# A cross-attention and expert layer on one core: the first six periods laid out anew, the router as one operand

## The chip, the core and the metric

One NeuronCore of a Trainium2 chip runs the whole program. The metric is the device time of the program in microseconds, the median over its runs; the kernel before takes 211.32 us (three runs: 210.55 to 213.79).

## What is computed

Eight sequences (batches) of 256 tokens, width 128, all in float32:

```python
scores = jnp.einsum('bhqd,bhkd->bhqk', q, k) / jnp.sqrt(jnp.float32(dh))   # 8 heads of 16
attn = jax.nn.softmax(scores, axis=1)                                     # over the heads
ctx = jnp.einsum('bhqk,bhkd->bhqd', attn, v)
...
logits = jnp.einsum('btd,de->bte', x, Wr) + br                            # 8 experts
topv, topi = jax.lax.top_k(logits, K)                                     # K = 2
gates = jax.nn.softmax(jnp.where(sel_mask, logits, neg_inf), axis=-1)
h = jax.nn.relu(jnp.einsum('btd,edh->bteh', x, W1) + b1)                  # hidden 256
out = jnp.einsum('bte,bteh,ehd->btd', gates, h, W2) + jnp.einsum('bte,ed->btd', gates, b2)
...
x = x + xattn(layernorm(x), context, context)
x = x + ffn(layernorm(x))
```

The softmax runs over the eight heads, not over the keys, so each pair of query and key has its own maximum and sum over 8 values. Every token goes through all eight experts; the gates of six are zero.

## The kernel before

Each batch's 256 tokens are two tiles of 128. Its attention is four units u = 0 to 3 (key tile by query tile). A unit is a chain over the engines: **scores** (TensorE, 1,024 columns into one of two PSUM pairs of banks), **head_max** (VectorE, maximum over the heads), **subtract_max** (TensorE adds minus the maximum to all heads in PSUM), **exponentiate** (ScalarE), **head_sum** (GpSimd, three additions; for the four units of batch 0 TensorE with eight identity matmuls, line 351), **invert_sum** (ScalarE, exp(-ln)), **normalize** (VectorE). After four units come **attend_values** (32 small matmuls), take_heads (ScalarE), **project_out**, then add_residual and ln2 (VectorE), ln2_end (GpSimd), make_x1n (ScalarE), **transpose_x1n** (TensorE), take_x1T_hi (ScalarE) and x1T_low (VectorE). With these come **route** (TensorE), take_logits, choose_experts, make_gates, transpose_gates (VectorE, gap_power on ScalarE), and eight times **expert_up** (six matmuls, line 403), relu (ScalarE), **expert_down** (eight, line 416), add_expert (VectorE), with gated_b2 and add_b2 once.

Scores, router and first expert layer use float32r, TensorE's reduced form, on a high and a low part (hi, lo) of one or both operands; three products stand for one float32 product. For the scores the parts of K and Q are spilled to DRAM and loaded again as stacks in which the parts of two heads lie under each other (k_stack, q_stack); batch 0 goes another way, with k_first and q_wide straight from PSUM (first_scores). SyncE's queue issues the spills, the loads of the stacks, w1, w2, most of the context and the stores of the output, strictly in the order written; each spill waits for both parts, each load for its spill. ScalarE's queue issues the attention's weights, the rest of x, two contexts and the small weights at the start.

The order of the work is written out by hand for each engine. Every engine runs its list strictly in order and waits on semaphores. The function beginning() of each engine holds the first six periods (0 to 5) as one list; from period 6 on period(i) (lines 418 onwards for TensorE) repeats a fixed pattern with the attention of batch i - 2, the end of that of i - 3, the experts 0 to 5 of batch i - 4 and 6 and 7 of batch i - 5. PERIODS is 13, and the last ones run out. The experts of batch 0 and of batch 1 up to 5 up, 4 down, and the attention up to unit 3 of batch 3 stand in beginning().

Other places that the change touches: keep_warm(n) (line 263) issues n dummy matmuls of 128 columns (each shows as two instructions on line 265) into the score bank of odd units. There are 12 of them ahead of beginning() and 5, 1 and 2 in its first lines. route (line 291) has three matmuls per token tile, each with the 128 tokens as weights and 8 columns of the router's weights (wr_hi or wr_lo) moving. ln1 (VectorE, line 833) makes mean and variance of a run of tiles, ln1_rstd_of and ln1_rest (GpSimd) the rest. GpSimd clears q_stack[1], v_pad and later q_stack[0] with memsets (lines 1223, 1224, 1187).

## Time and profile before

| | |
|---|---|
| median of three runs | 211.32 us (210.55 to 213.79) |
| profiled execution | 210.83 us, its span 209.0 us |
| TensorE matmul busy | 199.0 us, 95% of the span |
| TensorE weight load busy | 176.3 us, 84% |
| VectorE busy | 166.0 us, 79% |
| ScalarE busy | 132.3 us, 63% |
| GpSimd busy | 110.0 us, 53% |
| TensorE in the chain that ended last | 91% |

The span runs from the first to the last instruction of the program on the core. The chain that ended last is followed back from the last instruction, at each step to what released it. Ends of matmuls are modelled, since they are pipelined: a matmul group's distance from start to start is what it costs the ones behind it.

### The profile page before, as it was taken

How to read it: one execution, taken by the hardware profiler on the slowest of the kernel's cores; microseconds unless marked ns; L12 is line 12 of the kernel's file. 1: busy time of each engine (PE TensorE's matmuls, PEld its weight loads, DVE VectorE, ACT ScalarE, POOL GpSimd, SP SyncE). 2: the span in 40 equal slices, each digit the busy share in tenths (PEclk: the TensorE clock that was granted, in tenths of full speed). 3: DMA queues.
4: the chain of work that ended last, by engine and by line, in shares of the span. 5: the costliest groups of instructions: out<-in, count | busy, mean ns of one | idle time of the engine just before them, and what ended most of it. 6: DMA issues, size and time to landing. Idle time of an engine off the chain costs nothing.

```text
span 209.0 us, 4976 instructions
## 1 busy us (share of the span) xinstructions
PE 199.0 (95%) x1752; PEld 176.3 (84%) x1752; DVE 166.0 (79%) x445; ACT 132.3 (63%) x316; POOL 110.0 (53%) x132
## 2 busy tenths in 40 slices
PE   6999888698999999999999999999999999999994
PEld 6846775686899889997999799988998999789993
DVE  5398779889789999988888988798989978365542
ACT  2236847796578858687668767575767685345541
POOL 8603657869795475439661966285738672010000
PEclk9999999999999999999999999999999999999999
DMA  6549695725434233424241306050000000000000
GB/s 195 137 137 291 178 266 161 206 86 159 109 102 100 78 100 105 102 75 104 98 106 53 124 14 183 13 175 4 0 3 25 0 2 28 0 3 2 28 0 25
DMA packets 20248, 18.70 MB, mean 89 GB/s; under 512 B 1760, under 2 KB 18688, under 8 KB 20224
## 3 DMA queue, kind: packets, MB, share of 16 engines
q1 hardware_dynamic: 17472, 16.91, 28.2%
q10 hardware_dynamic: 2752, 1.48, 2.7%
q8 instruction: 14, 0.23, 0.4%
q14 instruction: 10, 0.08, 0.1%
HBM read 11.83 MB, written 6.55 MB: 88 GB/s over the span
## 4 chain that ended last, share of the span: by engine, by line
PE 91%; DVE 3%; ACT 2%; issue 1%; POOL 1%; DVEq 0%; POOLq 0%; ACTq 0%
PE y_ps L416 28%; PE h_ps L403 21%; PE score_ps L343 7%; PE misc_ps L362 6%; PE score_ps L331 6%; PE h_ps L351 4%; PE score_ps L265 3%; PE misc_ps L300 2%; PE misc_ps L383 2%; PE score_ps L320 2%; PE score_ps L403 2%; PE misc_ps L371 1%; PE misc_ps L270 1%; PE misc_ps L309 1%; PE misc_ps L289 1%
## 5 line engine op out<-in xcount | busy, mean ns | idle before, releaser
L670 ACT ACTIVATE hT<-h_ps,b_sb 128x256 f32<-128x256 f32 x118 | 49.4, 470 | 34.5 <-PE h_ps L403 33.4
L416 PE MATMUL y_ps<-w_sb,hT 128*128 128x128 f32 x512 | 68.4, 276 | 0.0
L416 PEld LDWEIGHTS y_ps<-w_sb,hT 128*128 128x128 f32 x512 | 63.3, 191 | 3.4 <-issue 2.0
L1152 POOL TENSOR_TENSOR half_sum<-e_sb 128x512 f32<-128x512 f32 x28 | 36.9, 1320 | 34.0 <-ACT e_sb L642 33.6
L911 DVE TENSOR_TENSOR attn<-e_sb,e_rcp 128x1024 f32<-128x1024 f32 x32 | 42.8, 1341 | 3.5 <-ACT e_rcp L653 3.3
L903 DVE TENSOR_REDUCE shift_m<-score_ps 128x128 fp32r<-128x1024 f32 x32 | 38.7, 1213 | 2.4 <-PE score_ps L331 1.2
L403 PE MATMUL h_ps<-x1T_hi,w_lo 128*128 128x256 f32 x118 | 37.7, 320 | 1.3 <-ACT hT L670 0.6
L642 ACT ACTIVATE e_sb<-score_ps 128x1024 f32<-128x1024 f32 x32 | 32.8, 1024 | 5.4 <-PE score_ps L343 5.2
L974 DVE SCALAR_TENSOR_TENSOR acc<-y_ps,gates,acc 128x128 f32<-128x128 f32 x96 | 29.0, 343 | 8.3 <-PE y_ps L416 6.9
L403 PE MATMUL h_ps<-x1T_lo,w_hi 128*128 128x256 f32 x118 | 33.1, 280 | 0.0
L403 PE MATMUL h_ps<-x1T_hi,w_hi 128*128 128x256 f32 x118 | 33.0, 279 | 0.0
L1154 POOL TENSOR_TENSOR quarter_sum<-half_sum 128x256 f32<-128x256 f32 x28 | 27.5, 982 | 2.2
L403 PEld LDWEIGHTS h_ps<-x1T_hi,w_lo 128*128 128x128 f32 x118 | 22.3, 189 | 4.3 <-issue 2.0
L403 PEld LDWEIGHTS h_ps<-x1T_lo,w_hi 128*128 128x128 f32 x118 | 22.4, 190 | 0.3
L403 PEld LDWEIGHTS h_ps<-x1T_hi,w_hi 128*128 128x128 f32 x118 | 22.3, 189 | 0.0
L343 PE MATMUL score_ps<-shift_m,neg_ident 128*128 128x512 f32 x64 | 21.5, 417 | 0.0
L331 PE MATMUL score_ps<-q_stack,k_stack 128*128 128x256 f32 x112 | 19.6, 299 | 1.1 <-issue 1.1
L1157 POOL TENSOR_TENSOR e_sum<-quarter_sum 128x128 f32<-128x128 f32 x28 | 16.6, 592 | 2.2
L1163 POOL TENSOR_TENSOR ln_rstd<-ln_var,neg_half 128x2 f32<-128x2 f32 x8 | 5.7, 708 | 21.2 <-DVE ln_var L870 21.2
L331 PEld LDWEIGHTS score_ps<-q_stack,k_stack 128*128 128x128 f32 x112 | 15.1, 190 | 1.5 <-issue 1.5
L362 PE MATMUL misc_ps<-attn,v_pad 128*32 128x256 f32 x256 | 15.5, 382 | 0.6 <-issue 0.6
L362 PEld LDWEIGHTS misc_ps<-attn,v_pad 128*32 128x32 f32 x256 | 7.7, 109 | 5.9 <-issue 1.0
(113 smaller groups left out, 286.8 us busy)
## 6 DMA issues: line engine op xcount, KB each, us to landing
k_scratch<-k_parts SPq DMA_DIRECT2D x14, 256.0 KB, 2.6
k_stack<-k_scratch SPq DMA_DIRECT2D x14, 256.0 KB, 4.0
q_stack<-q_scratch SPq DMA_DIRECT2D x28, 128.0 KB, 2.7
q_scratch<-q_parts SPq DMA_DIRECT2D x7, 256.0 KB, 2.5
w_sb<-in_w SPq DMA_DIRECT2D x1, 1024.0 KB, 6.5
out_y<-y_out SPq DMA_DIRECT2D x8, 128.0 KB, 1.9
x_all<-in_x ACTq DMA_DIRECT2D x1, 768.0 KB, 6.0
ctxT<-in_ctx_t SPq DMA_DIRECT2D x1, 640.0 KB, 5.5
```

The lines of the kernel that those rows point to most:

```text
L331: mm = nc.tensor.matmul(score_ps[:, u % 2, 2 * j * P:(2 * j + 2) * P], k_stack[:, b % 2, j, kt * P:(kt + 1) * P], q_stack[:, b % 2, j, :, ...
L343: mm = nc.tensor.matmul(score_ps[:, u % 2, half * BANK:(half + 1) * BANK], neg_ident[:], m4, start=False, stop=True, skip_group_check=True)
L362: mm = nc.tensor.matmul(misc_ps[32 * g:32 * g + 32, 0:S], v_pad[:, b % 4, kt, h, :], attn[:, b % 2, kt, h, :], start=(odd == 0 and kt == 0 ...
L403: mm = nc.tensor.matmul(hidden(j)[:, c * S:(c + 1) * S], w[:, e, c * P:(c + 1) * P], xt[:, b % 2, :], start=(k == 0), stop=(k == 2))
L416: mm = nc.tensor.matmul(y_ps[:, j % 2, t * D:(t + 1) * D], hT[:, j % 2, c, t * P:(t + 1) * P], w2_sb[:, e * HC + c, :], start=(c == 0), st ...
L642: nc.scalar.activation(e_sb[:, u, :], score_ps[:, u % 2, :], ACT.Exp, scale=SCALE).then_inc(exp_made, 1)
L670: op = nc.scalar.activation(hT[:, j % 2, c, :], hidden(j)[:, c * S:(c + 1) * S], ACT.Relu, bias=b1_sb[:, e * HC + c:e * HC + c + 1])
L903: nc.vector.tensor_reduce(shift_m[:, u % 2, :], score_ps[:, u % 2, :].rearrange("p (h q) -> p q h", h=H), AX.X, ALU.max).then_inc(max_made, 1)
L911: nc.vector.tensor_tensor(attn[:, b % 2, kt, :, qt * P:(qt + 1) * P], e_sb[:, u, :].rearrange("p (h q) -> p h q", h=H), e_rcp[:, u, :].uns ...
L974: op = nc.vector.scalar_tensor_tensor(out=dst, in0=y_ps[:, j % 2, t * D:(t + 1) * D], scalar=gates[:, b % 2, t, e:e + 1], in1=src[:, t, :] ...
L1152: nc.gpsimd.tensor_tensor(half_sum[:], e[:, 0:HQ // 2], e[:, HQ // 2:HQ], ALU.add).then_inc(sum_step, 1)
L1154: nc.gpsimd.tensor_tensor(quarter_sum[:], half_sum[:, 0:HQ // 4], half_sum[:, HQ // 4:HQ // 2], ALU.add).then_inc(sum_step, 1)
```

## The change

Router: wr_hi and wr_lo lie side by side in one tile wr_pair. For each token tile one matmul multiplies x1T_hi by both (16 columns), a second adds x1T_lo times the high part to the first 8. take_logits adds the two halves and the bias in two operations with a semaphore between (logits_step) where it had one. This holds for all batches.

SyncE's queue: w1 goes out ahead of every spill, behind two waits for inputs of ScalarE's queue; then both spills (K, Q) of a batch go ahead of both stack loads, for batches 1 and 2, and the rest of the context goes out between batch 1's loads and batch 2's spills.

beginning() is written anew on all four engines. On TensorE the dummies take their PSUM place and a wait as arguments, and stand in ten places behind the first twelve (27 dummies; before in three, 8). Batch 1's units stand wholly ahead of attend_values(0), and three units of batch 2 stand at least in part ahead of expert_up(0, 0). ln1 works on one batch at a time. GpSimd's memset of q_stack[1] moves behind the first ln1_rest. The shapes of k_first and q_wide get a dimension of 1, the counts of the waits stay the same in effect, and period(i) keeps its order.

```diff
 # route
-                    for k, (xt, w) in enumerate(((x1T_hi, wr_lo), (x1T_lo, wr_hi), (x1T_hi, wr_hi))):
-                        mm = nc.tensor.matmul(misc_ps[:, S + t * E:S + (t + 1) * E], xt[:, b % 2, tok], w[:],
-                                              start=(k == 0), stop=(k == 2), skip_group_check=True)
+                    nc.tensor.matmul(misc_ps[:, at:at + 2 * E], x1T_hi[:, b % 2, tok], wr_pair[:].rearrange("p k e -> p (k e)"),
+                                     start=True, stop=False, skip_group_check=True)
+                    mm = nc.tensor.matmul(misc_ps[:, at:at + E], x1T_lo[:, b % 2, tok], wr_pair[:, 0, :],
+                                          start=False, stop=True, skip_group_check=True)
 # take_logits
-                nc.vector.tensor_tensor(logits[:], misc_ps[:, S:S + TT * E].rearrange("p (t e) -> p t e", e=E),
-                                        br_sb[:].unsqueeze(1).to_broadcast([P, TT, E]), ALU.add).then_inc(logits_made, 1)
+                nc.vector.tensor_tensor(logits_part[:], parts[:, :, 1, :], br_sb[:].unsqueeze(1).to_broadcast([P, TT, E]),
+                                        ALU.add).then_inc(logits_step, 1)
+                dve.wait_ge(logits_step, b + 1)
+                nc.vector.tensor_tensor(logits[:], parts[:, :, 0, :], logits_part[:], ALU.add).then_inc(logits_made, 1)
 # SyncE
+            sp.wait_ge(x1_in, 16)
+            sp.wait_ge(ctx_in[1], 16)
+            sp.dma_start(w1_sb[:], w1.rearrange("e d h -> d e h")).then_inc(w1_in, 16)
             spill_k(1)
-            sp.dma_start(w1_sb[:], w1.rearrange("e d h -> d e h")).then_inc(w1_in, 16)
+            spill_q(1)
             load_k_stack(1)
-            spill_q(1)
             load_q_stack(1)
+            sp.dma_start(ctxT[:, 3:B, :], ...)
             spill_k(2)
-            sp.dma_start(ctxT[:, 3:B, :], ...)
+            spill_q(2)
             load_k_stack(2)
-            spill_q(2)
             load_q_stack(2)
```

TensorE's list, up to the first experts, as it stands after the change (kw is keep_warm):

```
project_k(0) project_v(0) kw(2) transpose_xn(0) kw(2) project_q(0) project_k(1) first_scores(0,0) project_k(2)
transpose_xn(1) first_scores(0,1) subtract_max(0,0) project_q(1) kw(3) first_scores(0,2) subtract_max(0,1)
head_sum(0,0) subtract_max(0,2) first_scores(0,3) head_sum(0,1) transpose_xn(2) subtract_max(0,3) project_v(1)
head_sum(0,2) scores(1,0) project_q(2) head_sum(0,3) project_v(2) subtract_max(1,0) scores(1,1) kw(2)
scores(1,2) kw(2) subtract_max(1,1) kw(2) subtract_max(1,2) scores(1,3) attend_values(0) scores(2,0)
subtract_max(1,3) project_out(0) kw(3) scores(2,1) subtract_max(2,0) project_k(3) kw(5) transpose_xn(3) kw(4)
transpose_x1n(0) scores(2,2) subtract_max(2,1) route(0) expert_up(0,0) project_q(3) scores(2,3)
subtract_max(2,2) expert_up(0,1) expert_down(0,0) attend_values(1) expert_down(0,1) project_out(1)
expert_up(0,2) project_k(4) kw(2) expert_up(0,3) expert_down(0,2) subtract_max(2,3) expert_up(0,4)
transpose_x1n(1) expert_down(0,3) scores(3,0) route(1) expert_up(0,5) project_v(3) ...
```

The same of VectorE (new), ScalarE (new) and GpSimd (new):

```
VectorE: ln1(1) spread_q(0,0) ln1_end(1) spread_q(0,1) head_max(0,0) k_lo(1) ln1(2) head_max(0,1) q_lo(1)
split_wr head_max(0,2) ln1(3) k_lo(2) ln1(4) head_max(0,3) normalize(0,0) normalize(0,1) head_max(1,0) q_lo(2)
normalize(0,2) normalize(0,3) head_max(1,1) head_max(1,2) ln1(5) head_max(1,3) normalize(1,0) head_max(2,0)
add_residual(0) ln2(0) head_max(2,1) k_lo(3) ln1(6) normalize(1,1) x1T_low(0) head_max(2,2) take_logits(0)
normalize(1,2) normalize(1,3) q_lo(3) choose_experts(0) make_gates(0) transpose_gates(0) add_expert(0,0)
add_residual(1) ln2(1) head_max(2,3) ... head_max(3,1) make_gates(1) transpose_gates(1) normalize(2,2)
add_expert(0,6) k_lo(5) normalize(2,3) add_expert(0,7) ...
ScalarE: take_xnT(0) take_v(0) take_k_first(0) take_k_hi(1) take_xnT(1) exponentiate(0,0) take_q_hi(1)
make_xn(2) take_k_hi(2) exponentiate(0,1) ... exponentiate(1,0) exponentiate(1,1) take_v(2) exponentiate(1,2)
invert_sum(1,0) split_w1(3) take_heads(0) exponentiate(1,3) invert_sum(1,1) take_k_hi(3) exponentiate(2,0)
make_x1n(0) invert_sum(1,2) take_xnT(3) take_x1T_hi(0) exponentiate(2,1) invert_sum(1,3) relu(0,0) ...
GpSimd: memset v_pad, iota, ln1_rstd_of(0), memset q_stack[0], ln1_rstd_of(1), ln1_rest(2), memset q_stack[1],
ln1_rest(3), ln1_rest(4), split_w1(0..2), head_sum(1,0) head_sum(1,1) head_sum(1,2) ln2_end(0) head_sum(1,3) ...
```

## Rows read from the trace of the kernel before

**Rows 1.** The page's strips of 40 slices: TensorE busy tenths, and its granted clock
```profile
PE   6999888698999999999999999999999999999994
...
PEclk9999999999999999999999999999999999999999
```

**Rows 2.** Busy time by stretch: stretch, its length, then each engine's busy us
```profile
9.38:39.06 29.68, 25.40 (x174) 18.09 (x175) 24.42 (x58) 17.37 (x40) 15.05 (x20) 1.00 0.73 202
39.06:81.44 42.38, 41.72 (x376) 36.99 (x377) 38.21 (x92) 31.05 (x76) 30.23 (x37) 1.00 0.39 114
81.44:209.00 127.56, 124.45 (x1160) 113.96 (x1158) 98.99 (x283) 81.42 (x198) 57.69 (x63) 1.00 0.17 48
```

**Rows 3.** TensorE's waits, 7 to 83 us: who waited for whom, total, times, longest
```profile
PE misc_ps L283 <- ACT x1n L596: 1.4, 1, 1.4
PE score_ps L331 <- issue: 1.1, 1, 1.1
```

**Rows 4.** Timeline of TensorE, a steady router: start, us, line, operation
```profile
86.03 0.25 PE L300 MATMUL misc_ps<-wr_lo,x1T_hi 128*128 128x8 f32 x1
...
86.70 0.37 PE L403 MATMUL h_ps<-x1T_hi,w_lo 128*128 128x256 f32 x1
```

**Rows 5.** VectorE's line 918, take_logits: ns min/median/max
```profile
L918 DVE TENSOR_TENSOR logits<-misc_ps,br_sb x8: 161/176/177, 41.7 to 191.3; 128x16 f32<-128x16 f32 x8
```

**Rows 6.** The page's groups: busy us and mean ns, idle before
```profile
L911 DVE TENSOR_TENSOR attn<-e_sb,e_rcp 128x1024 f32<-128x1024 f32 x32 | 42.8, 1341 | 3.5 <-ACT e_rcp L653 3.3
L903 DVE TENSOR_REDUCE shift_m<-score_ps 128x128 fp32r<-128x1024 f32 x32 | 38.7, 1213 | 2.4 <-PE score_ps L331 1.2
...
L642 ACT ACTIVATE e_sb<-score_ps 128x1024 f32<-128x1024 f32 x32 | 32.8, 1024 | 5.4 <-PE score_ps L343 5.2
```

**Rows 7.** Timeline of TensorE, the beginning
```profile
7.32 1.28 PE L265 MATMUL score_ps<-ident 128*128 128x128 f32 x10
...
23.37 1.95 PE L351 MATMUL h_ps<-e_sb,ident 128*128 128x128 f32 x16
26.41 0.71 PE L331 MATMUL score_ps<-q_stack,k_stack 128*128 128x256 f32 x4 [1.09 <-issue]
...
30.92 1.93 PE L362 MATMUL misc_ps<-attn,v_pad 128*32 128x256 f32 x32 [0.62 <-issue]
...
39.06 0.38 PE L403 MATMUL h_ps<-x1T_hi,w_lo 128*128 128x256 f32 x1 [0.47 <-DVE x1T_lo L875]
...
81.44 0.38 PE L276 MATMUL misc_ps<-ident,xn 128*128 128x128 f32 x2
```

**Rows 8.** Timeline of GpSimd
```profile
3.40 1.88 POOL L1224 MEMSET v_pad<- 128x2048 f32 x1
```

**Rows 9.** Timeline of VectorE, the beginning
```profile
4.98 0.31 DVE L843 TENSOR_SCALAR ln_var<-ln_mv 128x2 f32<-128x2 f32 x1
...
11.21 0.42 DVE L875 TENSOR_TENSOR k_parts<-h_ps,k_parts 128x256 fp32r<-128x256 f32 x1
...
71.22 1.25 DVE L943 TENSOR_SCALAR gap_exp<-gap_exp 128x2 f32<-128x2 f32 x1
```

**Rows 10.** Timeline of SyncE's queue: DMA issues
```profile
13.04 0.62 SPq L244 DMA_DIRECT2D w_sb<-in_w  x1
...
16.85 0.43 SPq L201 DMA_DIRECT2D q_scratch<-q_parts  x1
22.11 1.76 SPq L223 DMA_DIRECT2D q_stack<-q_scratch  x4
```

**Rows 11.** The page's DMA issues: KB each, us to landing
```profile
q_scratch<-q_parts SPq DMA_DIRECT2D x7, 256.0 KB, 2.5
```

**Rows 12.** TensorE in the chain that ended last: start, us, line, instructions
```profile
84.68 0.70 PE h_ps L403 x6
85.38 0.89 PE y_ps L416 x8
...
95.22 1.86 PE misc_ps L362 x32
```

More of the change, by code:

```diff
@@ L262, in _, with keep_warm @@
         def _(pe):
-            def keep_warm(n):
-                for _ in range(n):
-                    nc.tensor.matmul(score_ps[:, 1, 0:P], ident[:], ident[:], start=True, stop=True, skip_group_check=True)
+            def keep_warm(times, dst, freed, n):
+                wait(pe, freed, n)
+                for _ in range(times):
+                    nc.tensor.matmul(dst, ident[:], ident[:], start=True, stop=True, skip_group_check=True)
             def project_k(b, freed, n):
@@ L520, in beginning @@
-                expert_up(0, 0)
-                scores(2, 0)
-                route(0, x1T_lo_made, 1)
-                expert_up(0, 1)
-                subtract_max(1, 3)
-                project_k(3, logits_made, 1)
-                expert_down(0, 0)
-                expert_up(0, 2)
+                keep_warm(2, y_ps[:, 0, 0:P], q_lo_made, 1)
+                subtract_max(1, 2)
+                scores(1, 3)
+                attend_values(0, v_taken, 3)
+                scores(2, 0)
+                subtract_max(1, 3)
@@ L541, in beginning @@
                 subtract_max(2, 2)
-                project_out(1, b2_added, 1)
+                expert_up(0, 1)
+                expert_down(0, 0)
+                attend_values(1, q_lo_made, 3)
+                expert_down(0, 1)
+                project_out(1, heads_taken, 2)
+                expert_up(0, 2)
+                project_k(4, x1_made, 2)
+                keep_warm(2, y_ps[:, 0, 0:P], gated, 1)
+                expert_up(0, 3)
+                expert_down(0, 2)
+                subtract_max(2, 3)
@@ L543, in beginning @@
+                expert_up(0, 4)
+                transpose_x1n(1, k_lo_made, 4)
                 expert_down(0, 3)
+                scores(3, 0)
+                route(1, x1T_lo_made, 2)
                 expert_up(0, 5)
-                project_k(4, x1_made, 2)
+                project_v(3, logits_made, 2)
                 expert_down(0, 4)
-                scores(3, 0)
+                gated_b2(0, v_taken, 4)
+                scores(3, 1)
+                transpose_xn(4, b2_added, 1)
                 expert_up(0, 6)
+                subtract_max(3, 0)
@@ L754, in beginning @@
+                split_w1(3)
+                take_heads(0)
+                exponentiate(1, 3)
+                invert_sum(1, 1)
+                take_k_hi(3)
+                exponentiate(2, 0)
+                make_x1n(0)
+                invert_sum(1, 2)
+                take_xnT(3)
+                take_x1T_hi(0)
+                exponentiate(2, 1)
+                invert_sum(1, 3)
+                relu(0, 0)
+                make_xn(4)
                 split_w1(4)
-                exponentiate(1, 0)
+                take_q_hi(3)
@@ L788, in beginning @@
+                gap_power(0)
+                take_heads(1)
+                invert_sum(2, 0)
+                relu(0, 2)
+                split_w1(6)
+                relu(0, 3)
                 take_k_hi(4)
                 make_x1n(1)
+                take_x1T_hi(1)
+                invert_sum(2, 1)
+                relu(0, 4)
+                split_w1(7)
+                exponentiate(2, 3)
+                take_v(3)
+                relu(0, 5)
+                make_xn(5)
+                take_xnT(4)
@@ L1110, in beginning @@
                 add_expert(1, 2)
-                k_lo(5)
-                normalize(3, 0)
                 add_b2(1)
-                head_max(3, 3)
+                normalize(3, 1)
                 add_expert(1, 3)
-                normalize(3, 1)
+                add_expert(1, 4)
                 x1T_low(2)
-                add_expert(1, 4)
             dve.wait_ge(ident_made, 1)
```

418 lines of the change are left out of this document (201 added, 217 removed).

## The prediction

> **What bounds the kernel now.** I began with the page's strip of 40 slices [rows 1]: TensorE's digit is below 9 in slices 1, 5 to 8 and 10 (5.2 us each) and in the last, the epilogue; all others hold a 9. The clock strip is 9 throughout, so no wait of today costs clock. The stretch table [rows 2] puts this in numbers: from the query projection of batch 0 (9.38) to the first expert matmul (39.06) TensorE is busy 25.40 of 29.68 us, from there to the start of period 6 (81.44) 41.72 of 42.38, and nothing but the 127.56 us of written-out periods follows. The waits [rows 3] name the largest holes: 1.4 us for x1n of batch 0 and 1.1 us ahead of scores(1, 0), listed as issue, where the stack loads had only just landed. Hence two levers. A beginning shorter by x moves all that follows by x; a period shorter by y gives 6y, since batches 2 to 7 are routed in the dense part.
>
> **The router.** Today six matmuls follow each other every 0.11 us, each with its own weight load: the first starts at 86.03, the expert behind the sixth at 86.70 [rows 4], 0.67 us in all. The new form needs four. That is 2 x 0.11 = 0.22 us per batch, 6 x 0.22 = 1.3 us over periods 6 to 11; the other two batches are inside the walk below. On VectorE take_logits becomes two dependent operations of about 0.18 us [rows 5], some 0.3 us more per period with the wait. I cost it at nothing: VectorE is busy for 98.99 us of the last 127.56 [rows 2], and at least one expert matmul group stands between route and the first TensorE instruction that waits for the logits. Without that cover it would cost 8 x 0.3 = 2.4 us.
> These matmuls have 8 columns. The Trainium skill, page "TensorE: Matmul & The Clock Gate", section "Wait — 56ns, not 53.3ns?", says that starts never come closer than about 25 ns however small a matmul is. Were that floor the price of a removed matmul, 6 x 2 x 25 ns = 0.3 us would be saved; the row says 110 ns, and the row decides.
>
> **The first six periods.** Nothing is computed less here, only order changes, so I walk the new queues: an instruction starts when the one ahead on its engine is out and what it waits for has ended, with today's times: head_max 1.2, normalize 1.3 (1.15 to 1.25 where nothing holds it), exponentiate 1.0 [rows 6], a head_sum on TensorE 1.8 from start to start, a dummy 0.22 (the five take 1.28 from the first start to the last modelled end, 1.1 from start to start) [rows 7].
>
> *To 10.6 us.* GpSimd now clears v_pad first and q_stack[0] right behind the first ln1_rstd. Today a memset from 3.40 to 5.28 [rows 8] lies over ln_var, which starts at 4.98 and ends at 5.29, where the memset does, 0.31 for two elements [rows 9]: a VectorE tensor_scalar waits for the memset. The new memset runs about 5.9 to 7.7 and holds xn of batch 0 till about 8.0. Today the five dummies from 7.32 on [rows 7] hide xn until 8.4, so the transposition comes at 8.1, 0.3 earlier, and the first scores at 10.6. Bounds for this step: the full 1.8 later or nothing; 0.3 earlier is taken.
>
> *The transfer queue.* k_lo(1) moves behind head_max(0, 0): 12.95 instead of 11.21 [rows 9], so its spill starts 1.7 us later. q_lo(1) ends at 16.0, 0.8 before today's spill of q at 16.85 [rows 10]. The weights w1, 1 MB, today go out at 13.04, and the q spill behind them lets the q stack load issue only at 22.11: 5.3 us for a transfer whose median is 2.5 [rows 10, 11]. In the new order w1 goes out at about 6, beside the rest of x. Today w1 and the q spill were both in 9.1 us after w1's issue, which bounds w1 at 15.1 then, before the q spill at 16.0; x of batch 2 is asked for at 13.3, and I take it as in. The q spill then takes 2.5, its four loads issue at 18.7 to 20.4 and land at about 23.2, against 26.4 today (4.3 behind the issue; 4.5 now). Every DMA here is on SP's queue: two k spills, one q spill, two k and four q loads, in the same number as before; ctx rest goes behind them, 2 us ahead of the need. POOL: the second memset at 15.5 to 17.3 will hold the CAST of split_wr by 1.3 us, and head_max(0, 2) behind it; subtract_max(0, 2) still starts at 18.8, as TensorE is at head_sum(0, 0) till then.
>
> *To attend_values(0).* TensorE reaches scores(1, 0) not at 23.2 but at 25.2, because head_sum(0, 2) is ahead of it: 1.2 us before today's 26.41. So two thirds of the DMA gain is hidden. Then three of batch 1's units are run ahead of attend_values(0), one VectorE maximum and one exponential after the other: subtract_max(1, 1) at 31.2, (1, 2) at 32.3, scores(1, 3) at 33.0 behind the exponential of (1, 1). attend_values(0) starts at 33.5, against 30.92 [rows 7]. The lead has become a lag of 2.6 us; the six dummies in between fill holes of 0.9, 0.5 and 0.5 us and cost nothing.
>
> *To expert_up(0, 0).* project_out(0) at 36.4, add_residual at 37.3, ln2 to 38.7, GpSimd to 39.7. ScalarE has two exponentials, an inversion and take_k_hi(3) ahead of make_x1n(0), which comes at 40.5; the x1n transposition also waits for take_xnT(3) and starts at 42.2. Scores(2, 2) and subtract_max(2, 1) follow, the router at 43.6, expert_up(0, 0) at 44.1, 5.0 us later than today's 39.06 [rows 7]. Twelve dummies lie in waits here (37 to 42.2, with two matmul groups between).
>
> *To period 6.* Work that stood behind the first expert is now ahead of it: three scores, three subtractions, project_k(3), the transposition of xn(3), a router, about 4.2 us. What is left is 14 ups of 0.70, 13 downs of 0.89, two attend_values of 1.86 [rows 12], five scores, five subtractions and the small ones: 35.2 us. Today the stretch has 39.3 us of such work in 42.4 [rows 2]. Following VectorE I find the new holes: 0.5 us for relu(0, 2), some 0.5 around the second x1n and its router, and 0.8 where expert_down(1, 0) waits for add_expert(0, 6) if make_gates(1) is held by a GpSimd sum as it is today at 71.22 (1.25 us for two elements [rows 9]). Period 6 starts at 81.9 with that hold and 81.1 without, today at 81.44 [rows 7]. I take the middle: no change.
>
> **The sum.** 0 for the beginning and -1.3 for the router, against the profiled execution's own 210.83 us (span 209.0 and 1.8 around it): 209.5. The median of the three runs is 0.5 above that execution, so the median comes out at **210.0 us**. Unknowns, by sides: a walk of 70 us in which each of some 15 hand-overs can be off by 0.2 either way: -3.0 to +2.2, ends that the first two rivals name.
>
> **Rivals.** *A, the holes do close.* The hand-overs may be quicker than I set them, above all between 29 and 42 us, where TensorE waits or runs dummies for 5 us. TensorE stands idle today for 4.28 and 0.66 us before period 6 [rows 2]; if the new order ends 3 of these 4.9, period 6 starts at 78.5 and the median is 207.0. For it: the gain of 3.2 us at the stacks is real. Against it: VectorE's own chain of maxima and products, not the transfer, sets the pace from 26 us on. It needs x1n ready by 39.
>
> *B, dummies in front of ready work, slower.* Behind the first twelve there are 8 dummies today and 27 after, 19 more at 0.22 = 4.3 us. They are in TensorE's queue whether or not there is a hole. The place is 29 to 42 us, with 18 of them. As long as the maximum or the x1n behind them comes later than the last dummy, they cost nothing; from that point each costs 0.22. If half of them are exposed, +2.1: 212.1; all: 214.3. Against it: my walk finds every hole longer than its dummies. A late x1n chain would cost alike.
>
> *C, the router gives nothing.* If the removed matmuls' weight loads hide under their neighbours, as far as the trace could mislead, or the longer logits chain takes the gain back, the median stays at 211.3. For it: the ends of these matmuls are modelled. Against it: starts 0.11 apart, and an expert that starts only behind the sixth. The floor in the page named above would make it 211.0.
>
> **How the numbers follow.** Forecast 0.50 (209.0 to 211.0 by itself), A 0.22, B 0.18, C 0.10. The range that leaves out 2 in 10 cuts A at its foot and B above its half: **206.8 to 212.8**. A difference under 2%, 4.2 us, can't be told from none; the runs shown spread over 3.2. Faster by over 2% means under 207.1: half of A, 0.10. Slower by over 2%, over 215.5, needs B whole and more: 0.03. Within: 0.87.
>
> **What would show it.** In the changed kernel's profile: the router's four starts 0.11 apart and periods of about 22.0 us instead of 22.2; first xn behind the memset at about 8; q stack load issued at about 18.7; scores(1, 0) at 25.2; attend_values(0) at 33.5; expert_up(0, 0) at 44.1; period 6 at 81.5. If TensorE has waits of its own in 29 to 42 us besides the dummies, B is wrong. I am wrong if attend_values(0) starts before 32, if the first expert starts before 42, or if a stack load is what TensorE waits for in batch 2 or 3.

## The result, and the profile after

The changed kernel takes **213.62 us** (four runs, 213.15 to 214.22) against 211.49 us of the kernel before (four runs, 210.55 to 213.79): ratio 1.0106, 95% interval 1.007 to 1.0143. Forecast were 210.0 us and a range of 206.8 to 212.8, so the kernel is about 1% slower where nothing or a little gain was expected. Its profiled execution took 213.15 us, span 211.1. One thing is needed to read the medians below: of the 111 executions of the kernel before that stand beside the experiments, 41 had a mean granted clock of 0.976 to 0.992 (medians of 213.0 to 213.8 us) and the others one of 0.997 and more, called "at full clock" here (medians of 211.1 to 211.5 us); the changed kernel showed none of the first kind in 14 executions, and at full clock it is 2.1 to 2.3 us behind.

The strip of 40 slices (tenths busy; engines and clock):

```profile
PE   6899999989899799999999999999999999999994
DVE  5689798989889998889888979898999887556532
PEclk9999999999999999999999999999999999999999
```

Against [rows 1] the dips of slices 5 to 8 are gone from TensorE's line, in part since the dummies there count as busy, but there is an 8 in slices 2, 9 and 11 and a 7 in slice 14, where the old kernel was full. The waits of TensorE from 7 to 86 us (by whom released: total, times, longest) say what those are:

```profile
PE y_ps L422 <- DVE acc L994: 1.1, 1, 1.1
PE misc_ps L274 <- DVE x L872: 1.0, 1, 1.0
PE misc_ps L287 <- ACT xnT L606: 0.4, 1, 0.4
```

The waits of [rows 3] are gone: the transposition of x1n now waits 0.4 us, for take_xnT(3), and scores(1, 0) for nothing. Two new ones on VectorE stand behind the first expert. The table of stretches, cut as in [rows 2] at the first query projection, the first expert matmul and period 6 (stretch and its length; busy time and count of PE, PEld, DVE, ACT, POOL; clock; DMA share; GB/s):

```profile
8.96:44.60 35.64, 34.29 (x238) 26.16 (x239) 30.76 (x61) 21.10 (x48) 20.75 (x29) 1.00 0.71 190
44.60:84.78 40.18, 37.95 (x352) 33.62 (x352) 37.42 (x94) 27.03 (x70) 28.15 (x38) 1.00 0.33 96
84.78:211.10 126.32, 123.18 (x1148) 112.69 (x1146) 98.98 (x289) 81.38 (x198) 57.61 (x63) 1.00 0.16 48
```

The written-out periods last 126.32 us instead of 127.56: -1.24. Period 6 begins at 84.78 instead of 81.44: +3.34. The sum, +2.1, is the difference of the two profiled spans. In the middle stretch TensorE is idle for 2.2 us, nearly all of it the two new waits (1.14 and 0.97), where before it was idle for 0.66, and VectorE is busy for 37.42 of 40.18: 93%, where before it was 38.21 of 42.38, 90%, with more work of batch 1 to 3 in it.

TensorE's timeline (start, us, line) at the places that the prediction named, forecast in its text as 25.2, 33.5, 42.2, 43.6 and 44.1:

```profile
25.34 0.71 PE L337 MATMUL score_ps<-q_stack,k_stack 128*128 128x256 f32 x4
...
33.87 1.93 PE L368 MATMUL misc_ps<-attn,v_pad 128*32 128x256 f32 x32
...
42.70 0.44 PE L287 MATMUL misc_ps<-ident,x1n 128*128 128x128 f32 x2 [0.45 <-ACT xnT L606]
...
44.16 0.25 PE L303 MATMUL misc_ps<-wr_pair,x1T_hi 128*128 128x16 f32 x1
44.27 0.25 PE L305 MATMUL misc_ps<-wr_pair,x1T_lo 128*128 128x8 f32 x1
44.38 0.26 PE L303 MATMUL misc_ps<-wr_pair,x1T_hi 128*128 128x16 f32 x1
44.49 0.25 PE L305 MATMUL misc_ps<-wr_pair,x1T_lo 128*128 128x8 f32 x1
44.60 0.36 PE L409 MATMUL h_ps<-x1T_hi,w_lo 128*128 128x256 f32 x1
```

The walk holds for 44 us within 0.6. Then comes the loss against it. VectorE and GpSimd side by side, first VectorE's timeline:

```profile
48.20 0.23 DVE L948 MAX8 top<-logits 128x8 f32<-128x8 f32 x2
48.47 1.16 DVE L951 TENSOR_TENSOR gap<-top 128x2 f32<-128x2 f32 x1
...
51.00 1.23 DVE L969 TENSOR_TENSOR gated_onehot<-onehot,gate_of 128x32 f32<-128x32 f32 x1
...
53.30 0.42 DVE L872 TENSOR_TENSOR x<-misc_ps,x_all 128x256 f32<-128x256 f32 x1
...
69.08 1.16 DVE L972 TENSOR_TENSOR gates<-gated_onehot 128x16 f32<-128x16 f32 x1
```

and GpSimd's:

```profile
48.32 1.29 POOL L1177 TENSOR_TENSOR half_sum<-e_sb 128x512 f32<-128x512 f32 x1
49.69 0.73 POOL L1179 TENSOR_TENSOR quarter_sum<-half_sum 128x256 f32<-128x256 f32 x1
50.49 0.45 POOL L1182 TENSOR_TENSOR e_sum<-quarter_sum 128x128 f32<-128x128 f32 x1
50.91 1.27 POOL L1177 TENSOR_TENSOR half_sum<-e_sb 128x512 f32<-128x512 f32 x1
...
68.93 1.29 POOL L1177 TENSOR_TENSOR half_sum<-e_sb 128x512 f32<-128x512 f32 x1 [1.93 <-ACT e_sb L657]
```

Read the ends. The gap of two elements per partition starts 0.15 us behind GpSimd's addition (48.32) and ends at 49.63; the addition ends at 49.61. The gated_onehot ends at 52.23, the addition that it met at 52.18; the gates at 70.24, theirs at 70.22. Each of these three is a VectorE tensor_tensor with both inputs in SBUF, takes about 0.2 us where nothing holds it, and here takes as long as the GpSimd addition beside it still does. Not every small operation is held: the reciprocal, with one input, took 0.17 us (50.58) inside GpSimd's e_sum of 50.49 to 50.94. Behind the first two of them in VectorE's queue stands add_residual(1) (x, 53.30), for which project_k(4) waits 0.97 us. Behind the third stand the additions of the experts, and expert_down(1, 0) waits 1.14 us for one at 72.77. The Trainium skill describes this in "SBUF — State Buffer", section "Who interferes with whom": VectorE and GpSimd share one pair of ports, a VectorE instruction with two SBUF inputs contends with a GpSimd instruction that reads SBUF, and the lock is held for the whole instruction. The trace agrees to 0.05 us at all three ends.

By groups, VectorE's lines of the middle stretch (line, tile, shapes, count, busy us, mean ns, idle before), after:

```profile
L928 DVE TENSOR_TENSOR attn<-e_sb,e_rcp 128x1024 f32<-128x1024 f32 x8 | 12.0, 1512 | 0.0
...
L951 DVE TENSOR_TENSOR gap<-top 128x2 f32<-128x2 f32 x2 | 1.8, 904 | 0.1
L969 DVE TENSOR_TENSOR gated_onehot<-onehot,gate_of 128x32 f32<-128x32 f32 x2 | 1.4, 710 | 0.1
L972 DVE TENSOR_TENSOR gates<-gated_onehot 128x16 f32<-128x16 f32 x2 | 1.3, 669 | 0.1
```

and before, in its stretch 39.06 to 81.44:

```profile
L911 DVE TENSOR_TENSOR attn<-e_sb,e_rcp 128x1024 f32<-128x1024 f32 x9 | 11.0, 1232 | 0.0
...
L931 DVE TENSOR_TENSOR gap<-top 128x2 f32<-128x2 f32 x2 | 1.1, 574 | 0.1
```

normalize takes 0.28 us more in each of eight, and of the small ones three now meet a GpSimd addition of 512 columns where before one took 1.25 us [rows 9] and one gap about 1.0 (mean 574 ns over two, 0.16 for the free one).

### The profile page after: what moved, and what is told of

Same layout as the page of the kernel before. It is cut to its first block, busy times and chain, and to the rows that moved or that the text cites. A ratio compares the mean times of both kernels' runs of the same rounds, so it can differ in the third digit from the quotient of the medians.

```text
span 211.1 us, 5045 instructions
## 1 busy us (share of the span) xinstructions
PE 202.5 (96%) x1774; PEld 179.1 (85%) x1774; DVE 172.7 (82%) x456; ACT 131.3 (62%) x316; POOL 111.9 (53%) x141
## 4 chain that ended last, share of the span: by engine, by line
PE 67%; DVE 5%; issue 2%; DVEq 0%
PE y_ps L422 25%; PE h_ps L409 18%; PE misc_ps L368 5%; PE score_ps L349 5%; PE score_ps L337 4%; PE misc_ps L389 2%; PE score_ps L409 2%; PE misc_ps L377 1%; DVE acc L994 1%; DVE shift_m L920 1%; PE misc_ps L314 1%; PE misc_ps L287 1%; PE misc_ps L274 1%; PE misc_ps L305 1%; PE misc_ps L293 1%
## 5 line engine op out<-in xcount | busy, mean ns | idle before, releaser
L1177 POOL TENSOR_TENSOR half_sum<-e_sb 128x512 f32<-128x512 f32 x28 | 35.8, 1278 | 31.3 <-ACT e_sb L657 30.9
L928 DVE TENSOR_TENSOR attn<-e_sb,e_rcp 128x1024 f32<-128x1024 f32 x32 | 45.3, 1421 | 1.0 <-ACT e_rcp L668 1.0
L1179 POOL TENSOR_TENSOR quarter_sum<-half_sum 128x256 f32<-128x256 f32 x28 | 31.2, 1113 | 2.2
L1182 POOL TENSOR_TENSOR e_sum<-quarter_sum 128x128 f32<-128x128 f32 x28 | 17.3, 618 | 2.2
L1188 POOL TENSOR_TENSOR ln_rstd<-ln_var,neg_half 128x2 f32<-128x2 f32 x8 | 5.6, 699 | 20.1 <-DVE ln_var L886 20.0
L1159 POOL TENSOR_TENSOR ln_rstd<-ln_var,neg_half 128x2 f32<-128x2 f32 x8 | 6.4, 806 | 13.2 <-DVE ln_var L859 13.1
```

What stands on the lines that cost most here:

```text
L928: nc.vector.tensor_tensor(attn[:, b % 2, kt, :, qt * P:(qt + 1) * P], e_sb[:, u, :].rearrange("p (h q) -> p h q", h=H), e_rcp[:, u, :].uns ...
L1177: nc.gpsimd.tensor_tensor(half_sum[:], e[:, 0:HQ // 2], e[:, HQ // 2:HQ], ALU.add).then_inc(sum_step, 1)
L1179: nc.gpsimd.tensor_tensor(quarter_sum[:], half_sum[:, 0:HQ // 4], half_sum[:, HQ // 4:HQ // 2], ALU.add).then_inc(sum_step, 1)
```

## The experiments

Two theories stood at first. **H**: GpSimd's long additions hold VectorE's instructions in the middle stretch, because the new order sets them beside each other. **B**, the rival from the prediction: the dummies cost TensorE's time. Others came later. All ratios are to the kernel before on the same chip. Executions at a lower clock are among those that they rest on; where these weigh, the medians at full clock stand beside the ratio.

**The router alone (e1_router).** The kernel before with wr_pair, the four matmuls and the two-step take_logits, and nothing else of the change.

> The kernel before with the router part alone (one operand, two-step take_logits, on all batches). Theory H (the loss lies in the new order of the first six periods, where GpSimd's instructions hold VectorE's; the router is a gain): the distance between two steady routers falls from 22.25 to 22.03 us and all eight batches gain 0.2: ratio to before 0.992 (209.8 us), range 0.990 to 0.995. Rival R (the longer logits chain on VectorE costs the gain back): ratio 0.998 to 1.003.

210.4 us, ratio 0.9918 [0.9884, 0.9952]. The distance of two steady routers goes from 22.25 to 22.03 us. At full clock 210.31 against 211.43: -1.1, where the expectation had 209.8 us; its ratio was met with the help of the slower executions of the kernel before. The term of the sum is right, and the price of a removed small matmul is 0.11 us (two per batch, 0.22 of the 22.25), as [rows 4] had it. The profiled execution also showed which premise of mine was wrong (stretches of the beginning, columns as above):

```profile
34.00:38.00 4.00, 2.07 (x17) 1.76 (x16) 3.69 (x10) 2.48 (x6) 2.78 (x6) 1.00 0.56 150
38.00:42.00 4.00, 3.54 (x19) 3.10 (x18) 2.73 (x4) 2.93 (x7) 3.34 (x4) 0.69 0.83 245
42.00:46.00 4.00, 4.00 (x27) 3.81 (x27) 3.06 (x13) 2.98 (x7) 1.12 (x3) 0.88 0.01 4
```

TensorE is busy for 2.07 of 4 us in the old order's hole ahead of the x1n, and then the granted clock is 0.69 and 0.88 of 2.4 GHz for 8 us: at the lower level for part of them. The profiled execution of the kernel before has the same hole and keeps its clock:

```profile
34.00:38.00 4.00, 2.07 (x17) 1.77 (x16) 3.69 (x10) 2.45 (x6) 2.80 (x6) 1.00 0.71 190
38.00:42.00 4.00, 3.52 (x27) 3.02 (x26) 3.26 (x6) 3.27 (x8) 3.34 (x4) 1.00 0.70 210
```

"No wait of today costs clock" was true of that execution, and not of 41 of the 111.

**The change without the 27 dummies behind the first 12 (e2_nodummy).**

```
             def keep_warm(times, dst, freed, n):
                 wait(pe, freed, n)
-                for _ in range(times):
+                for _ in range(times if times == 12 else 0):
```

> The changed kernel without the 27 dummies behind the first twelve; their waits stay. Theory H: each stood in a hole, so at most the two at 54.3 us and the two at 31 us give anything: 0 to -0.6 us, ratio to before 1.008 to 1.011. Rival D (dummies ahead of ready work): -2 to -4 us, ratio 0.99 to 1.00. Rival C (they keep TensorE's clock): slower than the changed kernel, with a granted clock below 1.0 in 29 to 42 us, ratio above 1.015.

214.45 us, ratio 1.0119 [1.0069, 1.017]: not faster, and five of six executions below a clock of 0.997; the one at full clock took 213.82. Its profile shows the fall at 45 us, just behind the holes that the dummies fill:

```profile
40.00:45.00 5.00, 2.47 (x15) 1.89 (x16) 4.05 (x10) 3.87 (x9) 4.42 (x6) 0.97 0.32 105
45.00:48.00 3.00, 3.00 (x13) 2.82 (x14) 2.79 (x5) 2.28 (x8) 0.00 (x0) 0.50 0.69 175
```

The lower clock could have hidden what the missing dummies give, so the places ahead of the fall decide: attend_values(0) starts at 33.86 us (with the dummies 33.87), scores(2, 1) at 38.18 (38.05), the first expert at 44.76 (44.60). B is refuted: the 25 dummies ahead of the first expert stood in holes. They cost nothing that can be seen, and hold the clock at 2.4 GHz where without them it is at 1.2 GHz for 3 us. How large the holes are, this kernel shows too, from scores(1, 1) to the transposition of x1n:

```profile
28.91:43.02 14.11, 9.14 (x71) 5.94 (x70) 12.79 (x26) 9.00 (x19) 11.71 (x13) 1.00 0.71 177
```

TensorE has 9.14 us of work in 14.11, VectorE 12.79.

**Short sums in the kernel after (e3_after_short).** This one, e4_before_short and e14_after_short_late leave four of the eight heads out of the sum.

```
-nc.gpsimd.tensor_tensor(half_sum[:], e[:, 0:HQ // 2], e[:, HQ // 2:HQ], ALU.add)
+nc.gpsimd.tensor_tensor(half_sum[:, 0:P], e[:, 0:P], e[:, P:2 * P], ALU.add)
...
-nc.gpsimd.tensor_tensor(quarter_sum[:], half_sum[:, 0:HQ // 4], half_sum[:, HQ // 4:HQ // 2],
+nc.gpsimd.tensor_tensor(quarter_sum[:, 0:P], half_sum[:, 0:P], e[:, 2 * P:3 * P],
...
```

> The changed kernel with the three additions of GpSimd's head_sum at 128 columns each, over four of the eight heads only; the other four are left out of the sum. GpSimd's instructions become 0.46 us long instead of 1.28, 0.74 and 0.46. Theory H (VectorE is the bound from 44 to 85 us and loses 6.8 us to holds by GpSimd there, 3.4 more than before the change): the holds shrink by more than half, period 6 starts 2 to 3 us earlier (82 to 83), ratio to before 0.995 to 1.001. Rival O (the order alone: too much attention ahead of the experts, holds are incidental): period 6 still starts after 84, ratio 1.007 to 1.011.

211.03 us, ratio 0.9963 [0.993, 0.9995], 2.6 us below the kernel after. Period 6 begins at 82.79, both new waits on VectorE are gone, and the groups are short again:

```profile
L928 DVE TENSOR_TENSOR attn<-e_sb,e_rcp 128x1024 f32<-128x1024 f32 x8 | 9.7, 1218 | 0.0
...
L951 DVE TENSOR_TENSOR gap<-top 128x2 f32<-128x2 f32 x2 | 0.7, 356 | 0.1
...
L972 DVE TENSOR_TENSOR gates<-gated_onehot 128x16 f32<-128x16 f32 x2 | 0.5, 248 | 0.1
```

**The same in the kernel before (e4_before_short)**, the control.

> The kernel before with the same shorter head_sum (four of eight heads, 128 columns). Control for the run above. Theory H: TensorE is the bound there and has little to win, 0 to -1.2 us, ratio 0.994 to 1.000, so that the distance between the two kernels shrinks from 2.1 us to under 1. Rival O: it gains as much as the changed kernel does and the distance stays at 2.

211.78 us, ratio 1.0012 [0.9965, 1.0059], just above the expected range, with five of twelve executions at a lower clock; at full clock 211.11 against 211.43. Short sums give the old order about 0.3 us, the new one 2.3 to 2.6. So most of what e3 gave back belongs to the new order. But a short sum is also an early sum: that was the next rival.

**Short additions, late sum (e14_after_short_late).** Two more additions of 128 columns, into columns that nobody reads, stand ahead of the last.

```
+nc.gpsimd.tensor_tensor(half_sum[:, P:2 * P], e[:, 4 * P:5 * P], e[:, 5 * P:6 * P], ALU.add).then_inc(pad_step, 1)
+nc.gpsimd.tensor_tensor(half_sum[:, 2 * P:3 * P], e[:, 6 * P:7 * P], e[:, 7 * P:8 * P], ALU.add).then_inc(pad_step, 1)
 pool.wait_ge(sum_step, at + 2)
+pool.wait_ge(pad_step, at + 2)
...
```

> The kernel after with the short head_sum of e3 (three additions of 128 columns over four of the eight heads) and between its second and third addition two more additions of 128 columns into a part of half_sum that nobody reads. So GpSimd's instructions are as short as in e3 (0.46 us each), but the sum comes after five of them, about 2.3 us, nearly as late as the full one (1.3 + 0.7 + 0.46 = 2.5 us). Theory H (long GpSimd additions hold VectorE's small instructions): the holds are short, period 6 begins at 82.8 to 83.5 us as in e3 (82.95), gap and gates on VectorE stay under 0.5 us, ratio to the kernel before 0.996 to 1.002. Rival L (what e3 gave back came of the sum's earlier arrival, the wait for log and reciprocal behind it): period 6 at 84.3 to 84.8 us as in the kernel after, ratio 1.006 to 1.010.

210.89 us, ratio 0.9976 [0.995, 1.0002]; period 6 at 82.39. From the first addition to the end of the sum (at 48 us) it takes 2.43 us (48.23 to 50.66), the kernel after 2.62 (48.32 to 50.94), e3 1.52. The lateness costs nothing; the length of the single instruction is what costs. The middle stretch of this kernel:

```profile
44.51:82.39 37.88, 37.76 (x352) 33.65 (x352) 33.35 (x94) 27.08 (x70) 27.40 (x51) 1.00 0.37 108
```

The same 352 matmuls and 94 VectorE instructions as after, in 37.88 instead of 40.18 us, and VectorE is busy for 33.35 instead of 37.42.

**The whole sum in short instructions (e16_after_split_sum).** Nothing is left out here: seven additions of 128 columns for one each of 512, 256 and 128.

```
+for j in range(4):
+    nc.gpsimd.tensor_tensor(half_sum[:, j * P:j * P + P], e[:, 2 * j * P:2 * j * P + P],
+                            e[:, 2 * j * P + P:2 * j * P + 2 * P], ALU.add).then_inc(sum_step, 1)
+for j in range(2):
+    pool.wait_ge(sum_step, at + 2 * j + 2)
+    nc.gpsimd.tensor_tensor(quarter_sum[:, j * P:j * P + P], half_sum[:, 2 * j * P:2 * j * P + P], ...
```

> The kernel after with head_sum over all eight heads as seven GpSimd additions of 128 columns instead of one each of 512, 256 and 128: nothing is left out, the longest instruction is 0.46 instead of 1.28 us, but the sum takes 7 x 0.42 + waits, about 3.2 us instead of 2.6. Theory H (the length of the GpSimd instruction holds VectorE's small ones): gap, gated_onehot and gates on VectorE at 0.2 to 0.5 us, period 6 at 82.4 to 83.3 us, ratio to the kernel before 0.996 to 1.002. Rival (the sum's time of arrival, or GpSimd's total of busy time beside VectorE, decides): period 6 at 84.8 us or later, since the sum comes 0.6 us later and GpSimd is busy for longer, ratio 1.009 to 1.014.

211.69 us, ratio 1.0012 [0.998, 1.0045], 1.7 to 1.9 us below the kernel after (213.36 in e10, 213.62). Period 6 at 83.02, though GpSimd is busy for more (33.11 of 38.08 us) and the sum at 48 us takes 3.12 us (48.73 to 51.85). The stretch, and its groups:

```profile
44.94:83.02 38.08, 37.91 (x353) 33.74 (x353) 34.10 (x94) 27.20 (x70) 33.11 (x65) 1.00 0.35 102
```

```profile
L928 DVE TENSOR_TENSOR attn<-e_sb,e_rcp 128x1024 f32<-128x1024 f32 x8 | 10.6, 1331 | 0.0
...
L969 DVE TENSOR_TENSOR gated_onehot<-onehot,gate_of 128x32 f32<-128x32 f32 x2 | 0.6, 300 | 0.1
L972 DVE TENSOR_TENSOR gates<-gated_onehot 128x16 f32<-128x16 f32 x2 | 0.6, 288 | 0.1
L951 DVE TENSOR_TENSOR gap<-top 128x2 f32<-128x2 f32 x2 | 0.6, 278 | 0.1
```

H is shown for 2.1 us (40.18 less 38.08), on a kernel that computes everything. It does not explain the whole loss: even so period 6 begins 1.6 us later than before (81.44).

**And the memsets of q_stack in four parts each (e17_after_split_both)**, on top of e16, for the 0.5 us by which the first expert starts late.

```
-nc.gpsimd.memset(q_stack[:, 1].bitcast(F32), 0.0).then_inc(q_zeroed[1], 1)
+for p in range(PAIRS):
+    nc.gpsimd.memset(q_stack[:, 1, p].bitcast(F32), 0.0).then_inc(q_zeroed[1], 1)
```

> As the kernel with the split sum, and each of GpSimd's two memsets of q_stack (2048 columns, 1.80 us) in four parts of 512 columns. Theory (these two hold the first xn, 1.86 us, and the CAST of split_wr, 1.16 us, and these the 0.5 us by which expert_up(0, 0) starts late): xn and CAST shorter than 0.9 us, expert_up(0, 0) at 44.0 to 44.2 us, period 6 0.4 to 0.5 us earlier than with the split sum alone, ratio 0.994 to 1.0. Rival (something else stands behind the late start, so the memsets cost nothing): expert_up(0, 0) at 44.5 to 44.9, ratio as with the split sum alone.

211.65 us, ratio 0.9984 [0.9954, 1.0015]: a median 0.04 us from that of e16. The CAST of split_wr fell from 1.16 to 0.34 us, and the median shows no gain from it; the pair of xn did not get shorter (1.97 us against 1.86), as the four memsets follow each other without a gap. So the medians speak against the CAST as the cause of the late start, and for xn the experiment says nothing. The trace can't settle it: it is of the slowest execution but one, waits 0.8 us at scores(1, 0), and its first expert starts at 46.15 us, outside both expectations.

```profile
6.09 1.97 DVE L864 TENSOR_SCALAR xn<-x_all,ln_mv,ln_rstd 128x128 f32<-128x128 f32 x2 [0.83 <-POOL ln_rstd L1159]
...
16.18 0.34 DVE L914 CAST wr_pair<-wr_sb 128x8 fp32r<-128x8 f32 x1
```

**One sum moved off GpSimd (e9_after_pe_sum).** head_sum(2, 0) on TensorE, in the place of four dummies; its invert_sum moves up in ScalarE's list too (not shown).

```
-    PE_SUMS = (0, 1, 2, 3,)
+    PE_SUMS = (0, 1, 2, 3, 8)
...
-                keep_warm(4, y_ps[:, 0, 0:P], q_lo_made, 1)
+                head_sum(2, 0, log_made, 4)
```

> The changed kernel with one head sum, that of unit 0 of batch 2, moved from GpSimd to TensorE in the place of the four dummies ahead of transpose_x1n(0), its invert_sum right behind that of unit 3 of batch 1. All work is done. GpSimd then has no 1.28 us addition while VectorE chooses experts and makes gates of batch 0 (gap 1.16 and gated_onehot 1.23 us in the changed kernel, 0.2 unheld). Theory H: those two are 0.2 to 0.3 us, the wait of 1.0 us of project_k(4) for x1 goes, period 6 starts 0.5 to 1.3 us earlier in spite of about 0.5 us more on TensorE and ScalarE ahead of the experts; ratio to before 1.000 to 1.006. Rival O (order alone): the wait stays, ratio 1.010 to 1.014.

214.28 us, ratio 1.0144 [1.0085, 1.0203], a miss. expert_up(0, 0) now waits 1.22 us for the sum's logarithm, since both share PSUM, and starts at 46.84; and the next GpSimd sum, (2, 1), now runs where (2, 0) did (50.55) and holds the gap as before (1.16 us), while gated_onehot is free (0.19). Inconclusive for H: the edit made a wait of its own.

**Without the exposed pair (e15_after_no_pair).** The kernel after less `keep_warm(2, y_ps[:, 0, 0:P], gated, 1)` behind project_k(4), the only dummies of the middle stretch.

> The kernel after without the pair of dummy matmuls that stands ahead of expert_up(0, 4) at 54.31 us, the only pair behind 44.6 us that its trace shows with no wait around it (0.37 us). Theory O (part of what is left of the loss is TensorE's own longer order): period 6 begins 0.3 to 0.4 us earlier than 84.78, ratio 1.007 to 1.008 to the kernel before. Rival (VectorE sets the pace of this stretch, so that a TensorE instruction taken away only makes the next wait longer): period 6 at 84.7 to 84.9 us, ratio 1.009 to 1.010.

213.75 us, ratio 1.0097 [1.0065, 1.0129], nothing gained against 213.62 and 213.36. In the traces the place of the pair is 0.55 us shorter (from project_k(4) to expert_up(0, 3): 0.35 us for 0.90), and the rest up to period 6 is 0.40 us longer (30.50 for 30.10). This agrees with VectorE setting the pace, though one trace of each is thin. Ahead of the pair TensorE's wait for x grew from 1.0 to 1.5 us; the edit can't be behind that, but a hold is: gates, at 52.84, met a GpSimd addition of 256 columns and took 0.76 us instead of 0.17. With this, period 6 begins at 85.79 us here, outside both expectations.

**The transfer queue alone (e5_queue).** The kernel before with SyncE's new order of w1, spills and loads.

> The kernel before with the new order of SyncE's queue alone (w1 first, both spills ahead of both loads, rest of the context behind batch 1's loads). Theory H: the stack of batch 1 is in at 23.8 instead of 26.3 us, so scores(1, 0) starts at 25.3 behind head_sum(0, 2) instead of 26.4, and most of that 1.1 us is handed on through head_sum(0, 3) to attend_values(0) and the first expert: period 6 0.5 to 1.1 us earlier, ratio 0.995 to 0.998. Rival V (VectorE's chain of maxima and products sets the pace from 27 us on): nothing is handed on, ratio 0.999 to 1.001.

210.34 us, ratio 0.9907 [0.9875, 0.9939], more than expected, as the ratio counts the slower executions of the kernel before; at full clock 210.34 against 211.35: -1.0, ratio 0.995. All 12 executions are at 0.997 and more, where the kernel before beside it had 9 of 23 below. Its own profiled execution still waited 0.35 us at scores(1, 0) (26.58; the four q loads took 2.91 us to issue) and is the slowest but one of the twelve, with period 6 at 81.59 us. So no trace shows where the 1.0 us arises.

**Queue and router (e6_router_queue), and these with 11 dummies in the old order's holes (e7_router_queue_fill).** The latter adds

```
+            def fill(n):
+                pe.wait_ge(q_lo_made, 1)
+                for _ in range(n):
+                    nc.tensor.matmul(y_ps[:, 0, 0:P], ident[:], ident[:], start=True, stop=True, skip_group_check=True)
```

at four places (2, 2, 5, 2) between 29 and 38 us.

> The kernel before with the router part and the queue part, beginning() as before. Theory H: the two add up, ratio 0.987 to 0.990 (209.0 us). Rival V: as the router alone, 0.991 to 0.993.

> The same with eleven dummies in the holes that the old order leaves on TensorE between 30 and 39 us (2 ahead of attend_values(0), 2 ahead of project_v(2), 5 ahead of transpose_x1n(0), 2 ahead of expert_up(0, 0)). Theory K (the lower clock that some executions show at 39 to 43 us comes from those holes): the granted clock is 0.997 or more in all executions, none is over 1.5 us above the fastest, ratio 0.982 to 0.987. Rival (the falls have another cause): executions at 0.99 and 0.984 stay, ratio as the one above.

209.78 us each, ratios 0.9899 [0.9854, 0.9944] and 0.9898 [0.9851, 0.9944], all executions at 0.998 and more. For e7 0.982 to 0.987 was expected, a miss. Both beat both kernels: 1.6 us below the kernel before at full clock (211.35), 3.6 to 3.8 us below the kernel after. With the queue in order the dummies add nothing. Period 6 of e7, and what follows it:

```profile
38.22:81.09 42.87, 41.94 (x374) 36.81 (x374) 38.72 (x94) 31.25 (x77) 31.61 (x37) 1.00 0.36 107
81.09:207.20 126.11, 123.01 (x1146) 112.53 (x1144) 98.92 (x289) 81.13 (x197) 58.61 (x63) 1.00 0.17 48
```

**Dummies alone (e8_fill).** The kernel before with 15 dummies: the same eleven, and four ahead of scores(1, 0). It tests whether the holes cause the lower clock.

> The kernel before with the same eleven dummies and four more ahead of scores(1, 0), nothing else. Theory K: the executions at a clock of 0.984 and below (about 12 in 30 of the kernel before, at 213 us and more) are gone, the executions at full clock stay at 210.5 to 211.6, spread under 1.5 us; median 211.0, ratio 0.995 to 0.999. Rival: dummies cost time, ratio 1.002 to 1.010, and slow executions stay.

211.6 us, ratio 1.0003 [0.9976, 1.003]: the median of all does not move, but none of 12 executions was under 0.997, against 9 of 23 beside it. That the holes let the clock fall is supported, but which hole is open: e5 and e6 keep the one of 34 to 38 us (TensorE busy for 2.07 of 4 us in both) and had no execution below 0.997 in 18. What they share with e8, in one profiled execution of each, is a fuller stretch from 24 to 29 us, where TensorE is busy for 4.65, 4.67 and 4.94 of 5 us, in the kernel before for 3.91. No run tests that stretch alone. Full-clock executions are 0.3 us slower with the dummies (211.61 against 211.35), which is within the spread.

**The kernel after once more (e10_after_again).**

> The changed kernel once more on the same chip, for a comparison with the run above and for the clocks of its executions. Both theories: ratio 1.008 to 1.013 against all executions of before, every execution at a granted clock of 0.997 or more.

213.36 us, ratio 1.0092 [1.0055, 1.013], all ten executions at 0.999 or 1.0. At full clock the kernel before takes 211.25 beside it: +2.1.

## Why the prediction was wrong

**The router: right.** Forecast -1.3 over the written-out periods, measured -1.24 (126.32 against 127.56); the longer logits chain cost nothing that shows. Rival C is refuted by e1; a price of 25 ns for a removed matmul would have left 0.3.

**To 10.6 us: right.** xn is held by the new memset (5.95 to 7.75) and ends at 7.9 (forecast 8.0); first scores at 10.51 (10.6).

**The transfer queue: right in size.** The q stack load issues at 18.11 (18.7), 4.0 us earlier than [rows 10], and scores(1, 0) starts at 25.34 (25.2), 1.1 us earlier, right behind head_sum(0, 2), which stands ahead of it in either order. Alone in the old order the queue is worth 1.0 us (e5). In the new order, as forecast, the walk from there to attend_values(0) spends the lead. What the old queue in the new order would take, no run shows.

```profile
5.42 0.37 SPq L246 DMA_DIRECT2D w_sb<-in_w  x1
...
16.07 0.34 SPq L202 DMA_DIRECT2D q_scratch<-q_parts  x1
...
18.11 1.91 SPq L224 DMA_DIRECT2D q_stack<-q_scratch  x4
```

**To attend_values(0), to expert_up(0, 0): 0.4 and 0.5 us late** (33.87, 44.60 for 33.5, 44.1). The first comes in small steps (subtract_max(1, 1) at 31.36 for 31.2, scores(1, 3) at 33.20 for 33.0). The cause is not settled; the median of e17 speaks against the CAST held by the second memset.

**To period 6: this step failed.** I forecast 37.4 us from 44.1 (81.9 with the hold of 0.8 us at expert_down(1, 0), 81.1 without); it took 40.18, 2.8 more. The step had two terms, TensorE's own work of 35.2 us and the waits.

*The work was counted too short.* TensorE's waits in the stretch are 1.14 and 0.97 us, so the instructions themselves take 38.07 us from start to start, not 35.2. With short sums, where no wait is over 0.1 us, the same 352 matmuls take 37.88 (e14). Read off the timeline, the 14 ups take 11.45 us instead of 9.8 (0.82 each, where [rows 12] has 0.70), the 13 downs 11.7 as forecast (11.6), the two attend_values 3.72, and the scores, subtractions and small ones 11.2 instead of 10.1. The hint was in my own check: by the same prices today's stretch came to 39.3 us of work in 42.4, but [rows 2] has TensorE busy for 41.72 there. And the sum was not added up right: 44.1, 35.2, twice 0.5 and 0.8 make 81.1 with the hold and 80.3 without it, so 0.8 of the 37.4 us has no term. Work 2.9 too short, waits 0.7 too short, 0.8 over: that is the 2.8.

*The waits were 2.1 us where I had 1.4, and other ones.* I had 1.0 us (relu(0, 2), and around the second x1n) and half of 0.8 more for the hold. The first two did not come. The hold did, as 1.14 us, and a second one that I did not have, 0.97 us at project_k(4), behind gap and gated_onehot. So the mechanism of the holds was in the prediction, and its extent was not: three small operations of the router (gap, gated_onehot, gates) are each held for about 1.0 us, and normalize takes 1.51 us in each of eight where I had 1.3, together some 4.7 us of VectorE's time. With short additions VectorE is busy for 4.1 us less (37.42 less 33.35, e14), and 2.1 to 2.3 of them came through to TensorE. What I did not do was lay GpSimd's sums of the new order beside VectorE's router chain, in a stretch where VectorE is busy for over 90%.

**Against the kernel before** the account is another one, and it closes: the first expert starts 5.54 us later (44.60 for 39.06), TensorE's instructions from there to period 6 take 3.66 less (38.07 for 41.73), its waits 1.46 more (2.11 for 0.65). That is +3.34, and -1.24 for the router. The holds are 2.1 to 2.3 of the 3.34, by experiment (e16: 40.18 less 38.08; e14: less 37.88). Some 1.0 to 1.2 us is the order itself: I forecast 5.0 us lost ahead of the first expert and 5.0 won back behind it, but only 3.66 of work had moved ahead, and even with no wait at all the stretch could not have won back more than 4.3.

**Rival B** would have given nearly the same number, 212.1 to 214.3 (its 19 dummies of 0.22 make 4.2, not 4.3), for another reason and is refuted (e2). That a median above 212 us stood in the text at all was luck, as the cause given for it did not act. **Rival A** did not come: even with the holds taken out, period 6 begins at 82.4 to 83.0 and not at 78.5. None of the signs that were named for being wrong showed, since all of them lay ahead of 44 us or in the loads, and the loss against the forecast lies behind it. And "no wait of today costs clock" fell for over a third of the executions of the kernel before. There the change does what it should: it has removed these executions, but so has the new queue alone.

**Still open**: the 0.5 us ahead of expert_up(0, 0), and what would make the new order with short whole sums (e16, 211.69) as quick as the old order with queue and router (e6, 209.78). In e16 TensorE has only 0.17 us idle in the middle stretch, so it is not lost there. It lies ahead of the first expert, which starts 5.8 us later than in e6 (44.94 for 39.13): between 29 and 43 us TensorE has 9.14 us of work in 14.11 while VectorE is busy for 12.79 (e2). That VectorE's chain sets the pace there is argued from these numbers and not tested.

## What to carry to other kernels

When a new order is walked, put the same prices on the old order's stretch first: here they gave 39.3 us where the trace had TensorE busy for 41.72, and the difference came back as the miss. Then set GpSimd's long instructions beside VectorE's small dependent ones: the hold costs the rest of the long instruction, and here cutting the long one into pieces gave most of it back even though the pieces take longer in all. An earlier transfer is worth what waits for it: try the queue alone in the old order first. And when a kernel's runs spread by more than 1%, compare their granted clocks, since one profiled execution may not be the one that pays for the holes.

## What the runs showed of the hardware

- A VectorE tensor_tensor on 2 to 32 elements per partition with both inputs in SBUF took 1.16 to 1.23 us when it started 0.09 to 0.15 us behind a GpSimd addition of 512 columns (1.27 to 1.29 us), 0.2 to 0.4 us beside additions of 128 columns (0.46 us). A reciprocal with one input took 0.17 us inside one of 128 columns.
- GpSimd memsets hold too: one of 2,048 columns (1.80 us) made a pair of VectorE's tensor_scalar xn take 1.86 us against 0.60 free, and a CAST of 8 columns 1.16; with the memset in four parts the CAST took 0.34, the xn, in its place behind the first part, 1.97.
- The hold works both ways: GpSimd's quarter_sum of 256 columns, 0.73 us free, took 1.60 beside a normalize (64.85 and 73.73 us, kernel after).
- After 4 us with TensorE busy for 2.07 of them (e1) the granted clock was 0.69 and 0.88 in the next two stretches of 4 us; after 5 us with 2.47 busy (e2) it was 0.50 for 3 us. The same 4 us with 2.07 busy were followed by 1.00 in the profiled executions of the kernel before and of e5. The clock falls in some executions of one and the same kernel (0.976 to 0.992 mean clock in 41 of 111 of the kernel before), and these took about 2.2 us longer.
